# A recurrent-attention block with a mixture of experts: another order of its front, shorter routing, values projected first

## The chip, the cores and the metric

The kernel runs on one core of one Trainium2 chip. The metric is the device time of one execution in microseconds (us), given as the median of three runs; lower is better. Engine names in this text: TensorE (PE in the profile, its weight loads PEld), VectorE (DVE), ScalarE (ACT), GpSimd (POOL), SyncE (SP). "ACTq", "SPq" and "POOLq" are the sequencers of these engines, which also issue DMAs.

## The reference

The input `x` is 4 batches of 512 tokens of 256 numbers. Every row is normalised (`xn`). From `xn` two things are computed and multiplied:

```
s: RMS norm, then q, k (128 wide), v, g (256 wide), gk = log_sigmoid(xn Wkg1 Wkg2 + b)/16
   16 heads: S_t = S_(t-1) * exp(gk_t) + k_t v_t ;  o_t = q_t S_t      (a scan over 512 tokens)
   o normalised per head, times silu(g), times Wo, added to xn
   RMS norm, then x + (silu(x W1) * (x W3)) W2                        (hidden width 704)
g: 16 experts (256 -> 224 -> 256, gated by silu), the 4 with the highest router scores
   weighted by their softmax; silu of the sum
out = x + s * g
```

The 2048 tokens times 4 experts are laid out in 80 tiles of 128 slots, so that one tile belongs to one expert.

## The kernel before, in words

**Engines as programs.** Each engine has a program of its own, in a fixed order, and the programs meet at semaphores. An engine that waits holds back everything that stands behind the wait. There is no planner: the order is written out by hand.

**Preparation.** SP loads the first batch and the weights `Wv`, `Wg`, `Wq`, `Wk` (L381 to L385), ACT issues the small loads (L606 to L618), all but three of them counted on one semaphore, `small_in`. ACT waits for all of `wa_in` and `small_in` (L621, L622), rounds the scaled weights to half precision (L626, "high part"), DVE computes what was lost (L898, "low part"); each product is then three half-precision products (`triple`, L312). DVE computes the norm factors of batch 0 (`statistics`, `scales`, L851 to L874), POOL makes the normed rows (L510), PE turns them (L1215), ACT and DVE split them into high and low part (L644, L912).

**Projections.** Each batch has eight outputs, in the order Z, K, V0, V1, LG, Q, G0, G1 (L295): decay, key, two halves of value, router scores, query, two halves of gate. Z is turned by ACT and POOL into the decay (L658 to L663, L515, L648); the values are copied by DVE (L927), stored to memory by SP (L407) and read back, repeated over key dimensions (L419, `vrep`, 512 KB for a step). `STEP_ENDS` (L302) says how many of the 24 outputs of batches 1 to 3 stand before the end of each of the eight steps of batch 0.

**The recurrence.** A batch takes eight steps. In step u DVE multiplies `vrep` by the key (L951), then runs two scans (L959); POOL multiplies by the query (`product`, L529); PE sums over the key (`read_out`, L1247). The scan of step u waits for the product of step u-2 (L955), the first of a batch for the banks that ACT fills with key and decay (`next_banks`, L711).

**Iterations.** The steps of batch 0 run beside the projections. Then `turns` (L338) runs iterations 1 to 5 of eight steps: in iteration i the recurrence of batch a = i, the norm chain of batch b = i-1 and the multilayer perceptron ("MLP") of batch c = i-2. The norm chain is: turned output (step 0), squares on ACT, head factors on DVE (step 2, L1109 to L1113), normalised output (step 3, L1116), turned back and gated (step 4), `Wo` (step 5), addition, row norms and their factors (step 6, L1125 to L1132), second norm, turned and split (step 7). The MLP has six gate-and-up steps (steps 0 to 5, L1291; multiplied by DVE in `gated`, L1074) and two halves of the product with `W2` (steps 6 and 7, L1279), added by DVE in the next iteration (`add_mlp`, L1086). In iterations 4 and 5 there is no recurrence; there ACT and DVE split the 16 experts' weights (L785, L1063), one for a step, the second waiting for the first.

**Routing.** DVE does it on 16 tiles of tokens by 16 experts, between the instructions of four recurrences (L975 to L1037): best scores (L987, L989), selection, softmax, counts by two matmuls (L1266), slot of each choice. For the slot of each of the four choices there are three instructions (L1032 to L1036). `name_tiles` (L1039) finds the expert of every tile, all 80 in one partition. POOL then scatters the rows to their slots (`scatter`, L556, 64 indirect DMAs), two for a step of iterations 1 to 4.

**Filling.** The slots have first to be filled with empty rows. ACT issues 16 DMAs (L634, L700), two for a step of batch 0, each of 640 rows of 1,096 bytes; POOL waits for them in front of the first scatter (L569).

**Experts.** 80 tiles, each turned, multiplied by gate and up, gated, turned, multiplied by down (L1362 to L1382), added to memory by POOL (L586). Then the last additions and the store. The diff does not touch this part or the end.

## Time and profile before

| | us |
|---|---|
| median of 3 runs | 574.86 |
| the runs | 574.86, 577.04, 572.45 |
| the profiled execution's own time | 574.92 |
| its span, first to last instruction | 572.9 |
| PE, DVE, ACT, POOL busy | 429.3, 345.0, 230.9, 304.7 |

The profile is of one execution. Busy times are means over very different stages, so a change in one stage has to be read from the rows of that stage. In a row of the timeline the columns are the start in us from the span's start, the busy time in us, the engine, the line of the code, the operation, output and inputs, and the count where several are merged; in brackets stands the idle time of the engine in front of it and what ended it.

### The profile page before, as it was taken

The page shows a single profiled execution, that of the slowest core. Times are in us where ns is not written, and L with a number is a line of the kernel's source. Part 1 is how long each engine was busy: PE and PEld are TensorE (multiplying, and loading weights), DVE is VectorE, ACT ScalarE, POOL GpSimd, SP SyncE. Part 2 cuts the span into 40 slices and gives each one's busy share as a digit, 9 for nine tenths or more (in the row PEclk, how much of TensorE's full clock was granted, in tenths as well). Part 3 has the DMA queues.
Part 4 walks back from the last instruction along what each step waited for, and adds up shares of the span by engine and source line. Part 5 has one row for each costly group of instructions (what it writes and reads, how often), then busy time and mean ns, then how long its engine had stood idle before and what let it go on. Part 6 is the DMA issues. An engine that isn't in the chain of part 4 may idle for free.

```text
span 572.9 us, 8861 instructions
## 1 busy us (share of the span) xinstructions
PE 429.3 (75%) x2170; PEld 254.9 (44%) x2171; DVE 345.0 (60%) x613; ACT 230.9 (40%) x521; POOL 304.7 (53%) x230
## 2 busy tenths in 40 slices
PE   2479970313568798699889989999999999999400
PEld 1134320101223354255465557767767767677200
DVE  4665867999989979985755633333333333333065
ACT  0526642300133132122554525556655656566221
POOL 4052695146768468576720006656566656666535
PEclk9989996655759899899999999999999999999855
DMA  8334998745535234232988845666666666664493
GB/s 265 110 111 160 304 330 279 270 150 171 186 123 185 89 126 151 106 114 65 357 288 238 176 149 85 112 101 114 103 112 112 112 102 110 111 85 57 55 318 121
DMA packets 78616, 90.42 MB, mean 158 GB/s; under 512 B 7704, under 2 KB 66808, under 8 KB 78584
## 3 DMA queue, kind: packets, MB, share of 16 engines
q1 hardware_dynamic: 47584, 54.82, 31.6%
q0 software_dynamic: 14592, 19.47, 20.0%
q10 hardware_dynamic: 16408, 15.73, 8.5%
q8 instruction: 16, 0.26, 0.2%
q14 instruction: 16, 0.13, 0.1%
HBM read 50.66 MB, written 39.34 MB: 157 GB/s over the span
## 4 chain that ended last, share of the span: by engine, by line
PE 54%; DVE 19%; issue 9%; DMA 8%; POOL 4%; ACT 2%; ACTq 2%; SPq 0%; POOLq 0%; DVEq 0%
PE mm_ps L315 33%; PE sum_ps L315 12%; DVE st L959 4%; PE turn_ps L1276 3%; DVE kv L951 3%; PE mm_ps L1374 3%; POOL qs L529 2%; DMA rows_scratch<-zrow 2%; DMA eb<-n_L_ffn_expert_bias_dram 2%; PE sum_ps L1247 2%; DVE w_gu L1181 2%; DMA vrep<-v_scratch 1%; DMA y_scratch<-y,X 1%; ACTq L636 1%; DVE ghead L1111 1%
## 5 line engine op out<-in xcount | busy, mean ns | idle before, releaser
L586 POOL DMA_INDIRECT y_scratch<-y,X x80 | 124.3, 1554 | 126.7 <-ACT y L815 96.6
L315 PE MATMUL mm_ps<-w_gu,xT 128*128 x480 | 103.9, 352 | 1.6 <-DVEq L1159 1.5
L529 POOL TENSOR_TENSOR qs<-st,q_sb 128x1024 f32<-128x1024 f32 x32 | 75.4, 2356 | 49.0 <-DVE st L959 24.3
L1071 DVE TENSOR_TENSOR xT<-turn_ps,xT 128x256 f16<-128x256 f32 x80 | 33.9, 425 | 88.0 <-ACT xT L726 88.0
L315 PE MATMUL sum_ps<-wd,hT 112*128 x320 | 82.4, 380 | 0.0
L558 POOL DMA_INDIRECT rows_scratch<-rows,slot_u x64 | 64.0, 1001 | 27.2 <-issue 15.1
L959 DVE TENSOR_TENSOR_SCAN st<-sum_ps,kv 128x512 f32<-128x512 f32 x64 | 75.1, 1210 | 1.0
L315 PE MATMUL mm_ps<-an2T,w 128*128 128x512 f16 x264 | 65.1, 403 | 13.6 <-DVE h_mlp L1080 11.1
L1247 PE MATMUL sum_ps<-qs,sumk 128*32 128x512 f32 x128 | 38.2, 710 | 38.5 <-POOL qs L529 37.2
L315 PEld LDWEIGHTS mm_ps<-w_gu,xT 128*128 128x128 f16 x480 | 46.6, 97 | 33.0 <-issue 2.7
L1164 DVE SCALAR_TENSOR_TENSOR h<-mm_ps,X,sl 128x224 f32<-128x224 f32 x80 | 36.1, 451 | 40.9 <-ACT sl L799 40.9
L315 PEld LDWEIGHTS sum_ps<-wd,hT 112*128 112x128 f32 x320 | 54.3, 190 | 4.7 <-issue 0.2
L815 ACT ACTIVATE y<-sum_ps,X 128x256 f32<-128x256 f32 x80 | 38.0, 474 | 44.3 <-PE sum_ps L315 44.3
L799 ACT ACTIVATE sl<-mm_ps,X 128x224 f32<-128x224 f32 x80 | 35.8, 447 | 43.4 <-PE mm_ps L315 43.4
L315 PE MATMUL mm_ps<-anT,w_a 128*128 128x512 f16 x168 | 43.0, 414 | 11.2 <-DVE anT L912 9.2
L315 PEld LDWEIGHTS mm_ps<-an2T,w 128*128 128x128 f16 x264 | 26.3, 103 | 54.1 <-issue 16.6
L315 PE MATMUL mm_ps<-w,h_mlp 128*128 128x256 f32 x192 | 47.8, 394 | 1.0 <-DVE h_mlp L1080 1.0
L951 DVE TENSOR_TENSOR kv<-vrep,mm_ps 128x1024 f32<-128x1024 f32 x32 | 38.8, 1212 | 5.6 <-ACT mm_ps L677 4.1
L315 PEld LDWEIGHTS mm_ps<-w,h_mlp 128*128 128x128 f32 x192 | 33.9, 189 | 14.5 <-issue 10.0
L732 ACT ACTIVATE sg<-mm_ps 128x512 f32<-128x512 f32 (+1 forms) x24 | 14.3, 597 | 46.8 <-PE mm_ps L315 46.8
L1276 PE MATMUL turn_ps<-ident,X 128*128 128x128 f32 x160 | 30.7, 274 | 2.5 <-issue 2.5
L315 PEld LDWEIGHTS mm_ps<-anT,w_a 128*128 128x128 f16 x168 | 16.9, 105 | 34.9 <-issue 17.8
(165 smaller groups left out, 533.4 us busy)
## 6 DMA issues: line engine op xcount, KB each, us to landing
vrep<-v_scratch SPq DMA_DIRECT2D x64, 256.0 KB
rows_scratch<-zrow ACTq DMA_DIRECT2D x16, 685.0 KB, 11.7
X<-rows_scratch SPq DMA_DIRECT2D x80, 137.0 KB, 2.6
w_gu<-y_scratch SPq DMA_DIRECT2D x16, 256.0 KB, 6.1
y_scratch<-zrow ACTq DMA_DIRECT2D x6, 640.0 KB, 5.9
w_gu<-in_L_ffn_gate_proj_dram SPq DMA_DIRECT2D x16, 224.0 KB, 6.8
w_gu<-in_L_ffn_up_proj_dram SPq DMA_DIRECT2D x16, 224.0 KB, 7.1
wd<-in_L_ffn_down_proj_dram SPq DMA_DIRECT2D x1, 3136.0 KB, 17.4
```

The source lines that it names most:

```text
L315: last = nc.tensor.matmul(out_ap, lhsT, rhs, start=(n == 0), stop=(n == len(pairs) - 1))
L529: nc.gpsimd.tensor_tensor(qs[:, u % 2, :, :], st[:, u % 2, :, :], pair_bc(q_sb[:, TOK(a)]), ALU.mult).then_inc(s["qs_ready"], 1)
L558: nc.gpsimd.indirect_dma_start(rows_dram, bass.IndirectOffsetOnAxis(ap=slot_u[:, j, t:t + 1], axis=0), rows[:, t, :], None).then_inc(s["sc ...
L586: nc.gpsimd.indirect_dma_start(y_dram[u % 2], bass.IndirectOffsetOnAxis(ap=X[:, u, TOKEN_C:TOKEN_C + 1].bitcast(U32), axis=0), y[:, u, :], ...
L799: nc.scalar.activation(sl[:, u % 2, :], M[u % 2][:, 0:I], ACT.Silu, scale=X[:, u, SCALE_C:SCALE_C + 1])\
L815: nc.scalar.activation(y[:, u, :], sum_ps[:, u % 2, 0:D], ACT.Copy, scale=X[:, u, bass.ds(e + WEIGHT_C, 1)])\
L951: nc.vector.tensor_tensor(kv[:, r, :, :], vrep[:, r, :, :], pair_bc(K_BANK), ALU.mult).then_inc(s["kv_ready"], 1)
L959: nc.vector.tensor_tensor_scan(st[:, r, j, :], A_BANK, kv[:, r, j, :], 0.0, ALU.mult, ALU.add).then_inc(s["st_ready"], 1)
L1071: nc.vector.tensor_tensor(xT[:, u % 2, 1, :, :].rearrange("p c n -> p (c n)"), PS[u % 2][:, 0:KC * P], xT[:, u % 2, 0, :, :].rearrange("p ...
L1164: nc.vector.scalar_tensor_tensor(out=h[:, u % 2, :], in0=M[u % 2][:, I:2 * I], scalar=X[:, u, SCALE_C:SCALE_C + 1], in1=sl[:, u % 2, :], o ...
L1247: last = nc.tensor.matmul(O0[rows_at:rows_at + QUARTER, :], sumk[:, off:off + QUARTER], qs[:, u % 2, j, :], start=(dd % PER == 0), stop=(d ...
L1276: last = nc.tensor.transpose(PS[u % 2][:, n * P:(n + 1) * P], X[:, u, n * P:(n + 1) * P], ident[:, :])
```

## The change

1. **Preparation.** The small loads are split over several semaphores and over SP and ACT: only `ln1` and three router and decay weights stay ahead on ACT; `bkg2`, `bg`, `ln2` and the expert bias go to SP's queue, the last two behind all of `x`. Weights are prepared in the order in which they are used, and PE waits for each output's own part. The outputs come in the order V0, V1, Z, K, LG, Q, G0, G1. ACT copies the values, not DVE. The norm factors of batches 2 and 3 move behind the first recurrence.
2. **Batch 0.** `STEP_ENDS` spreads the 24 outputs evenly. All eight recurrences stand ahead of the routing.
3. **Filling.** POOL prepares, in the space of the MLP weights, ten empty rows for each partition; ACT issues 8 DMAs (one for a step) of 128 pieces of 10,960 bytes in place of 16. The preparation of the MLP weights, whose space that is, moves on POOL from batch 0 to steps 0 to 5 of iteration 1, behind a wait for all fills, which stands behind the first product.
4. **Norm chain in six steps, MLP from step 6.** Head factors and normalised output are in step 1, gating in step 2, `Wo` and addition in step 3, row factors in step 4, turning and splitting in step 5. The MLP of batch b starts in step 6 of the same iteration; iteration 5 has six steps.
5. **Routing** in three parts (steps 0, 2 and 4 of iteration 1). The slots of the four choices are the four largest of 16 slot numbers: one multiplication and 16 instructions of maxima. The expert of tile p is found in partition p; one turn by PE and one copy bring the names to one partition.
6. **Scatters** begin in step 6 of iteration 1; two and three in turn in the steps of iterations 1 to 3, three for each step of iteration 4.
7. **Experts' weights**: one expert for a step until 7 are split, then two for a step.

```diff
-        Z_OUT, K_OUT, V0_OUT, V1_OUT, LG_OUT, Q_OUT, G0_OUT, G1_OUT = range(8)
+        V0_OUT, V1_OUT, Z_OUT, K_OUT, LG_OUT, Q_OUT, G0_OUT, G1_OUT = range(8)
-        STEP_ENDS = [7, 11, 14, 17, 20, 24, 24, 24]
+        STEP_ENDS = [4, 7, 10, 13, 16, 19, 22, 24]
+        MLP_FROM = 6
             for it in range(1, B + 2):
-                for u in range(U):
-                    step_fn(batch(it), batch(it - 1), batch(it - 2), u)
+                for u in range(U if it <= B else MLP_FROM):
+                    c, m = (it - 1, u - MLP_FROM) if u >= MLP_FROM else (it - 2, u + U - MLP_FROM)
+                    step_fn(batch(it), batch(it - 1), batch(c), m, u, (it - B) * U + u)
+        def experts_at(n):
+            single = n - 2
+            if 0 <= single < 7:
+                return (single,)
+            pair = 7 + 2 * (n - 9)
+            return tuple(e for e in (pair, pair + 1) if e < E) if n >= 9 else ()
 # gpsimd
+            step(nc.gpsimd.memset(wide, 0.0))
 ...
                 product(0, u)
-                if 1 <= u <= 3 * KC:
-                    mlp_weights((u - 1) // 3, (u - 1) % 3)
-            pool.sem_inc(s["prep_done"], 1)
+                if u == 0:
+                    pool.wait_ge(s["ln_ready"], 3)
+                if u < 2:
+                    for t in range((u + 2) * TPB, (u + 3) * TPB):
+                        normed_rows(t)
 ...
                     product(a, u)
                 if b == 0 and u == 0:
+                    pool.wait_ge(s["zero_fill"], 16 * FILLS)
+                    pool.wait_ge(s["late_in"], 32)
+                if b == 0 and u < 3 * KC:
+                    mlp_weights(u // 3, u % 3)
+                if b == 0 and u == 3 * KC - 1:
+                    pool.sem_inc(s["prep_done"], 1)
+                if b == 0 and u == SCATTER_FROM:
                     pool.wait_ge(s["route_ready"], 1)
-                    pool.wait_ge(s["zero_fill"], 16 * NT)
-                if b is not None:
-                    scatter(2)
+                if b is not None and (b > 0 or u >= SCATTER_FROM):
+                    scatter(3 if b == B - 1 or u % 2 else 2)
 # scalar
-            act.wait_ge(s["wa_in"], 64)
-            act.wait_ge(s["small_in"], 16 * NSMALL)
-            act.wait_ge(s["wv_ready"], 1)
+            act.wait_ge(s["ln1_in"], 16)
+            act.wait_ge(s["wqk_in"], 32)
 ...
+                if i in (V0_OUT, V1_OUT):
+                    c = i - V0_OUT
+                    act.wait_ge(vt_out[c], 16 * (p + 1))
+                    nc.scalar.activation(vt[:, c, :], bank_of(p, i), ACT.Copy).then_inc(s["vt_ready"], 1)
 ...
-                    zero(rows_dram[t * (SLOTS // NT):(t + 1) * (SLOTS // NT)], "zero_fill")
+                fill_rows(u)
 # vector
-            for c in range(1, B):
-                statistics(c)
 ...
-            scales(TPB, NT, TPB + NT)
+            statistics(1)
+            scales(TPB, 2 * TPB, 3 * TPB)
             low_rows(1)
 ...
-            FIRST = 6
+            FIRST = U
             for u in range(FIRST):
                 for _ in recurrence(0, u):
                     pass
+                if u == 0:
+                    row_scales(TPB, 2 * TPB)
+                    statistics(2)
+                    statistics(3)
+                if u == 1:
+                    scales(2 * TPB, NT, 6 * TPB)
+                    row_scales(2 * TPB, NT)
 ...
-            for j in range(TOP):
-                step(nc.vector.scalar_tensor_tensor(out=pick[:, :, :], ...
-                step(nc.vector.tensor_tensor(prod[:, :, :], pick[:, :, :], slot[:, :, :], ALU.mult))
-                step(nc.vector.tensor_reduce(slot_f[:, j, :], prod[:, :, :], AX.X, ALU.add))
+                step(nc.vector.tensor_tensor(slot[:, :, :], slot[:, :, :], Msel[:, :, :], ALU.mult))
+                for t in range(NT):
+                    nc.vector.max(s8[:, t, :], slot[:, t, :]).then_inc(s["dve_max"], 1)
 ...
+            def step_fn(a, b, c, m, u, n):
+                split_low(experts_at(n - 1)[-1:])
+                if b == 0 and u == 5:
+                    low_of_turned(b)
+                if a is not None:
+                    for ahead in {0: (0, 1), 1: ()}.get(u, (u,)):
+                        for _ in recurrence(a, ahead):
+                            pass
+                if c and u == MLP_FROM:
+                    add_mlp(c - 1, 1)
 ...
+                if c is not None and m < NF:
+                    gated(c, m)
```

## Rows read from the trace of the kernel before

**Rows 1.** Busy time by stage: start:end, length, PE, PEld, DVE, ACT, POOL, clock, DMA
```profile
0.00:40.70 40.70, 18.16 (x90) 9.01 (x91) 23.60 (x90) 13.03 (x22) 11.89 (x34) 0.98 0.53 163
40.70:127.00 86.30, 45.79 (x262) 19.06 (x264) 68.22 (x104) 33.87 (x56) 42.51 (x26) 0.78 0.74 250
127.00:165.80 38.80, 18.29 (x56) 7.30 (x56) 35.33 (x52) 6.18 (x17) 25.75 (x18) 0.59 0.52 165
165.80:215.50 49.70, 43.70 (x178) 20.83 (x179) 45.65 (x65) 12.98 (x27) 34.59 (x25) 0.90 0.38 129
215.50:264.90 49.40, 41.82 (x183) 20.76 (x182) 46.67 (x67) 12.00 (x25) 33.34 (x25) 0.97 0.35 111
264.90:307.00 42.10, 37.62 (x172) 22.74 (x172) 23.57 (x51) 17.65 (x31) 19.97 (x19) 1.00 0.83 267
307.00:336.40 29.40, 26.88 (x119) 15.37 (x119) 16.47 (x20) 12.39 (x17) 0.00 (x0) 1.00 0.67 155
336.40:572.90 236.50, 197.01 (x1116) 139.84 (x1116) 85.48 (x174) 122.82 (x326) 136.66 (x88) 0.93 0.63 119
```

**Rows 2.** The chain that ended last, stretch 0 to 130: start, us, what
```profile
6.98 9.39 DMA eb<-n_L_ffn_expert_bias_dram
...
60.57 8.04 DMA vrep<-v_scratch
...
97.99 12.98 DMA rows_scratch<-zrow
```

**Rows 3.** Timeline of 0 to 75: first projections, factors of batches 1 to 3, first recurrence
```profile
23.25 7.92 PE L315 MATMUL mm_ps<-anT,w_a 128*128 128x512 f16 x24 [7.83 <-DVE anT L912]
...
23.31 4.01 DVE L854 BATCH_NORM_STATS2 bst<-xn 128x6 f32<-128x256 f32 x12
...
32.20 0.89 DVE L860 BATCH_NORM_AGGREGATE mv<-bst 128x2 f32<-128x6 f32 x12
...
36.33 0.42 DVE L872 SCALAR_TENSOR_TENSOR rows<-ctmp,nhalf 128x12 f32<-128x12 f32 x1
...
40.67 1.21 DVE L951 TENSOR_TENSOR kv<-vrep,mm_ps 128x1024 f32<-128x1024 f32 x1
```

**Rows 4.** Costliest groups of the page: count, busy, mean ns, idle before
```profile
L529 POOL TENSOR_TENSOR qs<-st,q_sb 128x1024 f32<-128x1024 f32 x32 | 75.4, 2356 | 49.0 <-DVE st L959 24.3
...
L558 POOL DMA_INDIRECT rows_scratch<-rows,slot_u x64 | 64.0, 1001 | 27.2 <-issue 15.1
```

**Rows 5.** Groups by line and form, whole span: DVE's expert splits and value copies
```profile
L1063 DVE TENSOR_TENSOR w_gu<-w_gu 128x896 f16<-128x896 f32 x16 | 17.4, 1086 | 3.2 <-ACT w_gu L785 3.2
...
L927 DVE COPY vt<-mm_ps 128x512 f32<-128x512 f32 x8 | 5.5, 689 | 9.5 <-PE mm_ps L315 9.5
```

**Rows 6.** Timeline of 75 to 127: routing on DVE, GpSimd's weights, a late bank
```profile
84.26 1.30 DVE L989 MAX8 m<-lg 128x8 f32<-128x16 f32 x16
...
92.19 2.85 POOL L539 TENSOR_TENSOR w<-w_raw,w 128x1408 f16<-128x1408 f32 x1
...
101.16 1.22 DVE L951 TENSOR_TENSOR kv<-vrep,mm_ps 128x1024 f32<-128x1024 f32 x1 [4.15 <-ACT mm_ps L677]
...
115.96 0.42 DVE L1033 SCALAR_TENSOR_TENSOR pick<-cnt,Msel 128x256 f32<-128x256 f32 x1
...
121.00 0.42 DVE L1036 TENSOR_REDUCE slot_f<-prod 128x16 f32<-128x256 f32 x1
```

**Rows 7.** Timeline of 120 to 300: end of routing, a stalled head factor, PE's steps
```profile
125.03 1.86 DVE L1047 TENSOR_SCALAR tile_expert<-own 1x80 uint32<-1x80 f32 x1
...
135.02 2.79 DVE L1111 TENSOR_SCALAR ghead<-ghead 128x64 f32<-128x64 f32 x1
...
182.49 0.20 DVE L1111 TENSOR_SCALAR ghead<-ghead 128x64 f32<-128x64 f32 x1
...
269.29 2.76 PE L315 MATMUL mm_ps<-an2T,w 128*128 128x512 f16 x12
...
291.98 5.93 PE L315 MATMUL mm_ps<-w,h_mlp 128*128 128x256 f32 x24
```

566 lines of the change are left out of this document (293 added, 273 removed).

## The prediction

> **What bounds the kernel now.** I read the busy times by stage first [rows 1]. The reader is to see three different kernels in them. From 336.4 on the expert tiles run (PE busy 197 of 236.5 us); the diff does not touch them, so I carry 236.5 us over. From 165.8 to 264.9 lie iterations 2 and 3: 49.7 and 49.4 us, DVE busy 45.65 and 46.67 of them, so VectorE sets their length, with PE (43.7, 41.8) just behind. From 264.9 to 336.4 PE is busy 37.62 of 42.10 and 26.88 of 29.40: there PE sets the time. What is left is the front. From 40.7 to 165.8 (125.1 us) DVE is busy 68.22 + 35.33 = 103.6 us and idle 21.5, while the clock falls to 0.59 because PE has nothing to do. Up to 40.7 nothing is full.
>
> The chain of waits shows why the start is late [rows 2]: the expert bias, issued at 6.98, lands at 16.37, and ACT and DVE wait for all small loads before they prepare any weight. PE projects from 23.25 on; the first recurrence starts at 40.67 [rows 3], after the factors of all twelve further tiles (32.20 to 36.75) and the turning of batch 1 (36.75 to 40.67). In routing, DVE once sits idle 4.15 us until ACT has filled the key bank [rows 6], since ACT is busy issuing fills.
>
> So the model is four terms: start to first recurrence; batch 0 with iteration 1; iterations 2 and 3; the tail up to the first expert tile. The sum is made against 574.92 us, the profiled execution's own time, which is the median (574.86).
>
> **Term 1, start to first recurrence.** Without the wait for the expert bias, what is still needed are the norm factors, the mean of `Wv` and the normed rows, which are there at about 12 in the timeline. Of the 6.9 us between 16.37 and 23.25 some 3.3 are left, since only the parts for V0 stand ahead: PE starts at about 15.3. Then come V0, V1, Z, K, LG. Four outputs took 7.92 us [rows 3]; five take 8.8: LG is read at 24.1. DVE adds constants and low parts (0.6), statistics of four tiles (4.01 / 3 = 1.3) and the factors (36.75 - 32.20 = 4.55, less two thirds of 0.89: 4.0), then the turning as before, 3.9. First recurrence at 33.9, against 40.67: **-6.8 us**. Bounds: at most -9.4 (the transfer that is waited for), at least -3 (SP now issues five further small DMAs ahead of the value store, and `vrep` may land late). I take -6.8, nearest to the rows. The copy of V by ACT costs nothing on the path: ACT was busy only 13.03 of 40.7.
>
> **Term 2, batch 0 and iteration 1.** What DVE loses and gains:
> - values, six copies in this stretch at 0.689 [rows 5]: -4.1;
> - slots: from 115.96 to 121.42 there are twelve instructions, 5.5 us; in their place one multiplication (0.42), 16 maxima (1.30, as for the scores) and three short ones (0.5) [rows 6]: -3.3;
> - names of tiles: 121.42 to 126.89, 5.5 us, in one partition [rows 7]; a copy of about 0.3 is left: -5.2;
> - statistics of batches 2 and 3: 4.01 x 2 / 3 = +2.7; their factors +4.6 [rows 3]; two `gated` more in iteration 1, +1.4.
>
> Busy: 103.6 - 12.6 + 8.7 = 99.7. Idle was 21.5. With 3 outputs for a step in place of 7, the idle of 4.15 for the bank gone and the routing no longer laid between recurrences, I stepped the programs: idle stays where batch 2's rows are normed, turned and split behind its late factors (about 4.5), at two score outputs (2.5) and once for PE's last outputs (3): 10. PE's work in batch 0 (38.1 busy of 42.3 before) is then as long as DVE's, so it may set some steps. Term 2 is 109.7 in place of 125.1: **-15.4 us**. Bounds: -21 (idle almost gone) and -7 (idle as before, plus one more stall).
>
> The new wait in this stretch is POOL's, for all fills, behind the first product of iteration 1 (at about 88). Queued behind it are the MLP weights (up to 2.85 each, [rows 6]) and the second product, which `read_out` and so PE's turn of the normalised output in step 2 need by about 100. The last fill is issued at about 81. One fill took 12.98 us before, behind a backlog [rows 2]; 81 + 13 = 94, so it is just hidden. From a landing at 97 on, each us costs one.
>
> Where a head factor starts beside a product it took 2.79 us, otherwise 0.20 [rows 7]; these stalls are in the busy time that I carry over. The Trainium skill says in "GPSIMD Engine Reference", Key points, that GpSimd shares its SBUF interfaces with VectorE and contends with instructions in a two-port mode or with two SBUF inputs. That agrees with those two rows, and it speaks against this change, which gives POOL more to do beside DVE (weights in iteration 1, 20 scatters for an iteration); one or two further stalls of 2.6 us would make the sum 3 to 5 us longer. That is inside my range.
>
> **Term 3, iterations 2 and 3.** DVE's work stays (46.2 on average). Three waits come in. First, in step 6 DVE adds the old MLP's second half and then wants the new MLP's first product, for which PE has waited on that very addition: 2.76 us for twelve matmuls [rows 7] plus silu, 3.1 in all with nothing between. Second, POOL: 8 products at 2.36 and 20 scatters at 1.00 + 0.25 [rows 4] are 43.9 us in place of 38.9. It is not the bound, but in steps with three scatters (6.1 us) the product comes late, `read_out` holds PE's turns behind it, and the chain loses about 3. Third, about 0.9 at the head factors, whose input now is needed one step earlier. What goes: the idle around the row factors is hidden behind a recurrence, already counted in using busy time only. An iteration is 46.2 + 3.1 + 3 + 0.9 = 53.2: for two 106.4 against 99.1, **+7.3 us**. Bounds: -2 (waits fall beside each other) and +19 (below).
>
> **Term 4, tail.** Before: 336.4 - 264.9 = 71.5. Two gate-and-up steps of the last but one MLP now lie in iteration 3, -5.5 (2 x 2.76). A half product of 5.93 [rows 7] no longer overhangs the last recurrence: -1.5. With two experts for a step, ACT and DVE in turn split for some 4.2 us (DVE's share 1.09 for each, [rows 5], ACT's about the same) in a step of 2.76: +3. The 21 scatters left at 1.27 end about 27 us in, long before the first rows are wanted. 67.5: **-4.0 us**. Bounds -7 and +3.
>
> **Sum.** -6.8 - 15.4 + 7.3 - 4.0 = -18.9: 574.92 - 18.9 = **556.0 us**. All lower bounds together give 535.5, all upper ones 587.
>
> **Rivals.**
> 1. *The waits of term 3 hide* (DVE has 3 us of idle in each iteration already, which could absorb them). Against it: the addition and the product in step 6 depend on each other directly. Iterations of 49.5: 556.0 - 7.3 = 548.7. Chance 0.2.
> 2. *GpSimd paces iterations 2 and 3.* If the four extra scatters of an iteration (5 us) lie in full on the path beside the waits, an iteration is about 59: +19 in place of +7.3, so 567.7. For it: products already wait in turn with DVE and PE (49.0 idle in all, [rows 4], half of it for DVE). Chance 0.12.
> 3. *The front gives little*: weights arrive no earlier, or the first recurrence waits for `vrep`, which once took 8.04 us beside fills [rows 2]. Term 1 is nothing: 562.8. Here the change does not do what it says. Chance 0.08.
> 4. *The fills come late* (the slower side). The eight fills have pieces ten times as long, and no row shows such pieces. If each took the 12.98 us of the last one before [rows 2], one after another from 37 on, the last would land at 141, 44 us after the point where it decides (97): about 600. It makes the kernel slower than before from a landing at 116 on. Against it: 16 fills were served in the same stretch at 250 GB/s [rows 1], overlapping. Chance 0.05. The Trainium skill ("DMA: Bandwidth & Descriptors", Queues, rings and completion order) says that each DMA engine takes turns between queues packet by packet; by that, long packets would hold back `vrep`, not themselves.
>
> **How the numbers follow.** Forecast as summed, 0.55; the rivals 0.2, 0.12, 0.08, 0.05. The likeliest case gives 556.0, its own range is 547 to 565. To leave out no more than 2 in 10, I take 543 to 569: it holds rivals 1 to 3. A measurement of this kernel tells about 1% from no change (569.1 and below is faster, 580.6 and above slower). Faster: nearly all of forecast and of rivals 1 and 3, most of rival 2: 0.87. Within 1%: 0.07. Slower: rival 4 and an unseen wait, 0.06.
>
> **What would show it.** Right: the first recurrence starts at 32 to 36; iteration 2 starts (third batch's first key product) at 138 to 148; its length is 51 to 55, with DVE idle some 3 us before `gated` of m = 0; the first expert matmul is at 311 to 323; fills land before 97 and ACT no longer waits while issuing them. Wrong: a POOL wait of over 10 us for the fills, the first recurrence after 38, iterations of 58 or more, or PE at the low clock through batch 0.

## The result, and the profile after

The changed kernel takes 594.94 us (median of 4 runs, 593.17 to 596.18) where the kernel before takes 573.65 in the same measurement: 1.036 times as long, 95% interval 1.030 to 1.042. The forecast was 556.0, range 543 to 569. The profiled execution took 596.18 us, its span is 594.0 (before 572.9).

The windows of the changed kernel, cut at the same events as [rows 1]: first recurrence, first recurrence of batch 1, of batch 2, of batch 3, end of batch 3's, last MLP, first expert product.

```profile
0.00:34.30 34.30, 18.47 (x90) 8.96 (x91) 18.19 (x71) 14.51 (x26) 12.45 (x30) 0.95 0.72 202
34.30:94.00 59.70, 45.56 (x242) 18.00 (x242) 39.10 (x67) 31.06 (x56) 24.45 (x18) 0.85 0.72 269
94.00:166.20 72.20, 32.66 (x98) 12.89 (x98) 60.51 (x122) 12.88 (x26) 32.77 (x17) 0.62 0.43 130
166.20:224.80 58.60, 46.19 (x187) 23.70 (x187) 48.59 (x67) 13.12 (x28) 38.51 (x29) 0.91 0.42 125
224.80:282.90 58.10, 46.85 (x186) 23.70 (x186) 48.61 (x66) 11.94 (x26) 38.39 (x29) 0.88 0.36 109
282.90:319.40 36.50, 30.15 (x134) 18.96 (x134) 19.20 (x43) 13.56 (x26) 23.20 (x23) 0.95 0.88 295
319.40:357.50 38.10, 31.78 (x120) 18.57 (x121) 18.20 (x22) 15.16 (x20) 0.00 (x0) 0.87 0.65 148
357.50:594.00 236.50, 196.65 (x1116) 139.51 (x1113) 86.01 (x175) 122.91 (x326) 136.67 (x88) 0.93 0.65 119
```

Read the length of each line (second number) and VectorE's busy time (the third of the busy times). In the four terms of the prediction:

| term | before | forecast | measured |
|---|---|---|---|
| 1: start to first recurrence | 40.7 | -6.8 | 34.3: -6.4 |
| 2: batch 0 and iteration 1 | 125.1 | -15.4 | 131.9: +6.8 |
| 3: iterations 2 and 3 | 99.1 | +7.3 | 116.7: +17.6 |
| 4: up to the first expert product | 71.5 | -4.0 | 74.6: +3.1 |

The expert part is 236.5, as before. Term 1 came as forecast. Term 2 is off by 22 us and term 4 by 7, both with the wrong sign; term 3 is off by 10. Of the signs that the prediction named, batch 2 starts at 166.2 (138 to 148 if right), an iteration takes 58 us or more (the sign of being wrong), and the first expert product is at 357.2 (311 to 323).

In term 2 VectorE is busy 39.10 + 60.51 = 99.6 us; 99.7 were forecast. So the sum of its instructions was right, and the whole error is idle time: 32.3 us, not 10. Its waits from 34.3 to 166.2, longest first:

```profile
DVE kv L1013 <- DMA vrep<-v_scratch: 15.4, 4, 7.2
DVE h_mlp L1141 <- issue: 7.2, 1, 7.2
DVE anT L970 <- ACT anT L686: 3.3, 2, 2.5
DVE lg L979 <- PE mm_ps L323: 3.2, 1, 3.2
```

The columns are: who, waiting for whom, total us, times, longest. The last two are the ones I had foreseen (4.5 and 2.5). The first two I had not. The first stands in the chain of what ended last, as long transfers:

```profile
61.61 15.80 DMA vrep<-v_scratch
79.30 10.74 DMA vrep<-v_scratch
91.93 8.06 DMA vrep<-v_scratch
```

A load of `vrep` that took 8.04 us once in [rows 2] now takes up to 15.80. The second is called "issue", which names nobody; the timeline around it does:

```profile
150.94 2.35 POOL L557 TENSOR_TENSOR qs<-st,q_sb 128x1024 f32<-128x1024 f32 x1 [12.98 <-DVE st L1021]
153.24 2.85 POOL L567 TENSOR_TENSOR w<-w_raw,w 128x1408 f16<-128x1408 f32 x1
156.50 4.88 PE L323 MATMUL mm_ps<-an2T,w 128*128 128x512 f16 x12 [14.30 <-POOLq L602]
161.48 0.69 DVE L1141 TENSOR_TENSOR h_mlp<-mm_ps,sg 128x512 f32<-128x512 f32 x1 [7.23 <-issue]
```

The last part of the MLP weights (L567) stands in GpSimd's program behind the product of step 5, that product behind a scan that VectorE reaches only after the slots of the routing, and PE's first MLP product behind the weights. PE has then been idle 14.30 us, and the granted clock of the next 4.9 us is 0.55, so most of them run at 1.2 GHz: twelve products take 4.88 us, not the 2.76 of [rows 7].

### The profile page after: what moved, and what is told of

It is laid out like the page before. It is cut to its first block, busy times and chain, and to the rows that moved or that the text cites. A ratio compares the mean times of both kernels' runs of the same rounds, so it can differ in the third digit from the quotient of the medians.

```text
span 594.0 us, 8877 instructions
## 1 busy us (share of the span) xinstructions
PE 448.3 (75%) x2171; PEld 264.3 (44%) x2172; DVE 338.4 (57%) x626; ACT 235.1 (40%) x531; POOL 306.4 (52%) x231
## 4 chain that ended last, share of the span: by engine, by line
PE 42%; DVE 22%; DMA 19%; issue 9%; POOL 4%; ACT 3%; SPq 1%; POOLq 0%; DVEq 0%; ACTq 0%
PE mm_ps L323 25%; DMA y_scratch<-y,X 10%; PE sum_ps L323 7%; DMA vrep<-v_scratch 7%; DVE st L1021 3%; DVE kv L1013 3%; POOL qs L557 2%; PE turn_ps L323 2%; PE turn_ps L1338 2%; PE mm_ps L1448 2%; DVE w_gu L1246 2%; PE sum_ps L1316 1%; DVE grow L263 1%; DMA w_gu<-y_scratch 1%; DVE h_mlp L1141 1%
## 5 line engine op out<-in xcount | busy, mean ns | idle before, releaser
L557 POOL TENSOR_TENSOR qs<-st,q_sb 128x1024 f32<-128x1024 f32 x32 | 75.1, 2350 | 80.9 <-DVE st L1021 80.5
L323 PE MATMUL mm_ps<-an2T,w 128*128 128x512 f16 x264 | 64.3, 398 | 16.8 <-POOLq L602 14.3
L1316 PE MATMUL sum_ps<-qs,sumk 128*32 128x512 f32 x128 | 41.6, 734 | 41.2 <-POOL qs L557 40.8
L587 POOL DMA_INDIRECT rows_scratch<-rows,slot_u x64 | 62.7, 979 | 16.9 <-issue 16.3
L323 PE MATMUL mm_ps<-w,h_mlp 128*128 128x256 f32 x192 | 55.7, 442 | 7.3 <-DVE h_mlp L1141 7.3
L323 PEld LDWEIGHTS mm_ps<-w,h_mlp 128*128 128x128 f32 x192 | 39.1, 218 | 24.0 <-DVE h_mlp L1141 9.8
L323 PE MATMUL mm_ps<-anT,w_a 128*128 128x512 f16 x168 | 45.8, 430 | 3.9 <-DVE anT L970 1.9
L1013 DVE TENSOR_TENSOR kv<-vrep,mm_ps 128x1024 f32<-128x1024 f32 x32 | 38.8, 1212 | 16.5 <-DMA vrep<-v_scratch 16.4
```

The costliest lines, as they stand in the source:

```text
L323: last = nc.tensor.matmul(out_ap, lhsT, rhs, start=(n == 0), stop=(n == len(pairs) - 1))
L557: nc.gpsimd.tensor_tensor(qs[:, u % 2, :, :], st[:, u % 2, :, :], pair_bc(q_sb[:, TOK(a)]), ALU.mult).then_inc(s["qs_ready"], 1)
L587: nc.gpsimd.indirect_dma_start(rows_dram, bass.IndirectOffsetOnAxis(ap=slot_u[:, t, j:j + 1], axis=0), rows[:, t, :], None).then_inc(s["sc ...
L1013: nc.vector.tensor_tensor(kv[:, r, :, :], vrep[:, r, :, :], pair_bc(K_BANK), ALU.mult).then_inc(s["kv_ready"], 1)
L1316: last = nc.tensor.matmul(O0[rows_at:rows_at + QUARTER, :], sumk[:, off:off + QUARTER], qs[:, u % 2, j, :], start=(dd % PER == 0), stop=(d ...
```

## The experiments

Each kernel was timed in the same set of runs as the kernel before. Unless said otherwise an edit is made to the changed kernel. In three of the five sets of runs the kernel before itself took 584 to 586 us instead of 572 to 576 (last section); there I compare by the trace up to the end of batch 3's recurrence, which that does not touch (the kernel before has 60.6, 64.6 and 49.7 in such a set). The table gives for each run the ratio and, in us, three lengths between starts of first key products (batch 0 to 1, 1 to 2, 2 to 3), and VectorE's wait for `vrep` in the first two. Each length is of one execution: e3, e5, e7 and e14, whose edits change nothing in batch 0, have 60.6 to 63.4 there where the changed kernel has 59.7, and 131.6 to 133.0 for the first two lengths together (changed 131.9). So a difference of a few us in one length is read together with the waits, not alone.

| run | ratio (95%) | 0 to 1 | 1 to 2 | 2 to 3 | vrep wait | before took |
|---|---|---|---|---|---|---|
| before | 1 | 60.5 | 64.6 | 49.7 | 0.7 | |
| changed | 1.036 (1.030-1.042) | 59.7 | 72.2 | 58.7 | 15.4 | 573.7 |
| e1 | 1.039 (1.035-1.043) | 60.3 | 71.7 | 58.9 | 4.6 | 572.5 |
| e2 | 1.030 (1.025-1.036) | 60.4 | 66.7 | 59.4 | 15.4 | 572.5 |
| e3 | 1.040 (1.036-1.043) | 60.6 | 71.2 | 58.4 | 15.5 | 572.5 |
| e4 | 1.007 (1.005-1.010) | 63.3 | 68.6 | 51.0 | 16.2 | 572.5 |
| e5 | 1.032 (1.023-1.040) | 60.7 | 70.9 | 54.0 | 15.5 | 585.8 |
| e6 | 1.017 (1.009-1.025) | 55.3 | 62.1 | 58.5 | 10.9 | 585.8 |
| e7 | 1.040 (1.032-1.049) | 63.4 | 69.6 | 58.2 | 16.2 | 585.8 |
| e8 | 1.001 (0.998-1.005) | 55.2 | 64.7 | 49.7 | 10.5 | 585.8 |
| e9 | 1.003 (1.000-1.005) | 55.2 | 60.3 | 58.3 | 1.9 | 576.0 |
| e10 | 1.033 (1.028-1.037) | 61.0 | 71.6 | 58.6 | 9.3 | 576.0 |
| e11 | 0.993 (0.991-0.996) | 54.9 | 60.6 | 53.4 | 2.2 | 576.0 |
| e12 | 0.986 (0.980-0.992) | 54.6 | 62.8 | 51.4 | 0.4 | 576.0 |
| e13 | 0.990 (0.986-0.994) | 51.3 | 63.6 | 51.0 | 2.2 | 585.8 |
| e14 | 1.057 (1.053-1.061) | 63.1 | 69.7 | 57.9 | 15.9 | 585.8 |
| e15 | 0.999 (0.996-1.002) | 49.3 | 65.1 | 49.6 | none | 585.8 |
| e16 | 1.010 (1.007-1.013) | 49.9 | 61.1 | 54.2 | none | 585.8 |
| e17 | 0.994 (0.992-0.997) | 49.1 | 65.0 | 49.5 | 0.7 | 583.5 |

### Late vrep: size of the pieces, or order of the queue

```diff
-            nc.gpsimd.iota(wide_token.bitcast(I32), pattern=[[1, WIDE], [0, 1]], base=0,
-                           channel_multiplier=WIDE).then_inc(s["wide_slot"], 1)
+            nc.gpsimd.iota(wide_token.bitcast(I32), pattern=[[0, WIDE], [0, 1]], base=0,
+                           channel_multiplier=1).then_inc(s["wide_slot"], 1)
...
-                act.dma_start(rows_dram[i * P * WIDE:(i + 1) * P * WIDE].rearrange("(p n) c -> p (n c)", p=P), wide)\
+                act.dma_start(rows_dram[i * P * WIDE:(i + 1) * P * WIDE].rearrange("(n p) c -> p n c", p=P),
+                              wide.rearrange("p (n c) -> p n c", c=ROW))\
```

> The changed kernel takes 594.9 us. Edit: the eight fills write the same 11.2 MB, but as 1,280 pieces of 1,096 bytes each in place of 128 pieces of 10,960. Theory A (long pieces on ACT's queue hold back the loads of vrep on SP's queue): DVE's wait for vrep up to the end of routing, 15.4 us in the changed kernel, falls to 5 or less, the first recurrence of batch 2 starts 9 to 12 us earlier (at 154 to 157 in place of 166.2), the time is 583 to 586. Rival B (the bytes alone count, or the loads are late because SP's queue stands behind the stores of v): the wait stays within 3 us of 15.4 and the time within 3 us of 594.9. Rival C (the pieces cost the queues more than the bytes): fills land later, POOL waits for them in iteration 1, and the time is 598 or more.

Measured: the wait for `vrep` fell from 15.4 to 4.6 us, as theory A had it, and the time did not move: 595.27. Part of that fall is hidden behind the bank below; in front of the recurrences of batch 0 alone, which stand ahead of it, the wait fell from 12.6 to 4.6, and the last of them starts at 82.4 in place of 90.1. Three rows of this run's timeline, of ACT's queue and of VectorE:

```profile
81.48 8.49 ACTq L673 DMA_DIRECT2D rows_scratch<-w  x1
90.12 4.12 ACTq L673 DMA_DIRECT2D rows_scratch<-w  x1
95.11 1.22 DVE L1014 TENSOR_TENSOR kv<-vrep,mm_ps 128x1024 f32<-128x1024 f32 x1 [9.09 <-ACT mm_ps L724]
```

One issue of 1,280 pieces held ACT's queue 8.49 us (0.34 with long pieces; the first four issues of this run, with as many pieces, took 0.4, so it is those behind a backlog that are held), and the key bank that ACT fills was 9.09 us late. The same 11.2 MB cost VectorE's loads with long pieces and the issuing engine with short ones. That is also what [rows 6] showed before: 4.15 us for the same bank, where single issues of fills held ACT's queue up to 4.90 us. A part of rival C came too: the fills landed in 14.6 us (median, 8.4 with long pieces), and GpSimd waited 8.8 us for them in iteration 1. So A's mechanism held, its time did not.

```diff
             for u in range(U):
                 load_values((u + 2) // U, (u + 2) % U)
-                for p, i in outs_at(u):
+                for p, i in outs_at(u - 1) if u else ():
                     if i in (V0_OUT, V1_OUT):
                         store_values(p, i - V0_OUT)
```

> Edit: the changed kernel, with SP storing the values of a step's outputs behind the next step's loads of vrep, not ahead of them. Theory A (the fills on ACT's queue make vrep late): the wait for vrep up to the end of routing stays at 13 to 17 us in place of 15.4, the ratio at 1.034 to 1.038. Rival B (the loads stand behind stores that wait for their projection): the longest wait, 7.2 us in front of the sixth recurrence, goes, the wait in all falls to 8 or less, the ratio to 1.020 to 1.026.

Measured: 1.033 (1.028 to 1.037). The rows of its waits look like rival B at first:

```profile
DVE kv L1013 <- DMA vrep<-v_scratch: 9.3, 3, 7.0
DVE kv L1013 <- DMA v_scratch<-vt: 6.4, 1, 6.4
```

but together they are 15.7, and the time stays: with the loads ahead, the store comes late and the load behind it. So this order does not give the wait back. As the edit itself delays the stores, it does not rule the order out as a share; what speaks against that is e9 below, where the wait goes to 1.9 us with the order as it was.

Next, the fills in a space of their own, in pieces of middle size, with the weights back in batch 0; then the same, spread.

```diff
-    FILLS = 8
-    WIDE = SLOTS // (P * FILLS)
+    FILLS = 10
+    WIDE = 2
...
-        wide = w13[:, :, :, :].rearrange("p a c n -> p (a c n)").bitcast(F32)[:, 0:WIDE * ROW]
+        wide = fill1[:, 0:WIDE * ROW]
...
-                act.dma_start(rows_dram[i * P * WIDE:(i + 1) * P * WIDE].rearrange("(p n) c -> p (n c)", p=P), wide)\
+                act.dma_start(rows_dram[i * P * 8:(i + 1) * P * 8].rearrange("(n p k) c -> p n (k c)", p=P, k=WIDE),
+                              wide.rearrange("p (a c) -> p a c", a=1).to_broadcast((P, 4, WIDE * ROW)))\
...
+                if 1 <= u <= 3 * KC:
+                    mlp_weights((u - 1) // 3, (u - 1) % 3)
```

> Edit: the empty rows come from a space of their own (two rows for a partition), in ten fills of 512 pieces of 2,192 bytes, one for each step of batch 0 and two in iteration 1; with that, GpSimd prepares the MLP weights in batch 0 again and waits for the fills only before the first scatter. Theory A (two prices, each its own: 15 us of late vrep by the long pieces, of which the smallest pieces gave back 11 but paid 9 for a key bank behind ACT's blocked issues; and 5 us by the late MLP weights, which the run with two parts for a step gave back): the pieces of middle size keep most of the first without blocking ACT, the first recurrence of batch 1 starts at 84 to 88 in place of 94, that of batch 2 at 150 to 156 in place of 166, the time is 579 to 586. Rival B (ACT's queue is blocked by 512 pieces too, or the bytes alone make vrep late): only the weights' part comes back, 588 to 591. Rival C (GpSimd's weight work beside batch 0 costs DVE stalls and late products there): 591 or more.

Measured: batch 1 starts at 88.2, batch 2 at 150.3, both where theory A put them; `vrep` still costs 10.9 us. The absolute time, 595.8, lies outside A's 579 to 586, but from the last recurrence to the experts this run takes 94.9 us where the changed kernel, in a quiet set, takes 78.4; without these 16.5 us it would be 579.3 (an estimate from these figures). The ratio is 1.017. Not all of theory A is shown by it: its edit changes size, source and place at once, and only the parts' sum is measured.

```diff
-                fill_rows(u)
+                if u in (0, 1, 3, 5, 7):
+                    fill_rows((0, 1, 3, 5, 7).index(u))
...
+                if b == 0 and u < 5:
+                    fill_rows(5 + u)
```

> Compared by the ratio to the kernel before (changed kernel 1.036, narrow version 1.017), since the runs of a job share its runs. Edit: the narrow version, with five of its ten fills in batch 0 (steps 0, 1, 3, 5, 7) and five in steps 0 to 4 of iteration 1. Theory A (what is left of late vrep, 10.9 us, is the fills' bytes beside the loads): that wait falls to 4 or less, the first recurrence of batch 1 starts at 82 to 85 in place of 88.2, that of batch 2 at 144 to 148 in place of 150.3, the ratio is 1.005 to 1.010. Rival B (vrep is late because SP issues it behind the stores of v): the wait stays at 9 to 11 and the ratio at 1.017. Rival C (the fills of iteration 1 hold the first scatter, and POOL the next products): batch 2 starts later than 150.

e9 is e6 with this edit. Measured: 1.003 (1.000 to 1.005), the wait for `vrep` 1.9 us, batch 2 at 150.0. In front of the recurrences of batch 0 the wait fell from 4.2 to 0.5: the bytes beside the loads made it. The rest of e6's wait (6.5 us at the start of batch 1) is partly hidden here by the next row in the list; e13, without that row, has 2.2 in all. But batch 1 did not start earlier (89.7), because of that row:

```profile
DVE kv L1016 <- ACT mm_ps L723: 5.4, 1, 5.4
DVE lg L982 <- PE mm_ps L323: 4.1, 2, 3.3
```

The key bank again: ACT's program has it behind the last gate outputs, for which PE is late. By the first two lengths e9 gains 0.1 + 1.8 us on e6; the ratios differ by more (0.014), but come from unlike sets.

### The weights' wait

```diff
-                if b == 0 and u < 3 * KC:
-                    mlp_weights(u // 3, u % 3)
-                if b == 0 and u == 3 * KC - 1:
+                if b == 0 and u < 3:
+                    mlp_weights(2 * u // 3, 2 * u % 3)
+                    mlp_weights((2 * u + 1) // 3, (2 * u + 1) % 3)
+                if b == 0 and u == 2:
```

> Edit: POOL prepares the MLP weights of two parts in each of the steps 0 to 2 of iteration 1, in place of one in each of steps 0 to 5. Theory A (PE's first MLP product waits 14.3 us for the last part, and DVE's first gated product 7.2 us behind it): both waits go but for the 3 us that any first product costs there, the first recurrence of batch 2 starts 4 to 6 us earlier, the time is 589 to 591. Rival B (the product of the query that now comes later in steps 0 to 2 holds back PE's turned output and the head factors, and the loss only moves): the time stays within 2 us of 594.9. Rival C: PE's first MLP product waits for something else just as long (the turned and split rows of batch 0), the start of batch 2 does not move.

Measured: 589.79, and batch 2 at 160.6 in place of 166.2. This is theory A. PE's product now waits for the rows' low part:

```profile
148.60 4.73 PE L323 MATMUL mm_ps<-an2T,w 128*128 128x512 f16 x12 [5.12 <-DVE an2T L1154]
155.44 0.66 DVE L1142 TENSOR_TENSOR h_mlp<-mm_ps,sg 128x512 f32<-128x512 f32 x1
```

### Iterations 2 and 3

In the changed kernel VectorE's waits of iteration 3 (224.8 to 282.9) and GpSimd's are:

```profile
DVE xn L1194 <- PE turn_ps L323: 3.8, 2, 2.7
DVE h_mlp L1141 <- PE mm_ps L323: 2.9, 1, 2.9
DVE xn L1148 <- PE mm_ps L323: 1.0, 1, 1.0
...
POOL qs L557 <- DVE st L1021: 18.0, 6, 4.3
```

GpSimd waits for VectorE 18.0 us, so it does not pace the iteration. The 2.9 are the wait that I forecast at 3.1. But idle time is not all. VectorE is busy 48.6 us in each of the two iterations, where I had taken 46.2, and 2.1 of these 2.4 us are one small instruction of the row factors that starts beside a GpSimd product and ends with it (without a product beside it: 0.17):

```profile
260.45 2.35 POOL L557 TENSOR_TENSOR qs<-st,q_sb 128x1024 f32<-128x1024 f32 x1 [3.46 <-DVE st L1021]
260.54 2.28 DVE L263 TENSOR_SCALAR grow<-grow 128x4 int32<-128x4 int32 x1
```

The experiments took one of the waits at a time.

```diff
-                        for _ in recurrence(a, ahead):
-                            pass
-                if c and u == MLP_FROM:
-                    add_mlp(c - 1, 1)
+                        for k, _ in enumerate(recurrence(a, ahead)):
+                            if k == 0 and c and u == MLP_FROM:
+                                add_mlp(c - 1, 1)
+                if a is None and c and u == MLP_FROM:
```

> Edit: in step 6 the addition of the old MLP's second half stands between the multiplication and the two scans of that step's recurrence, not behind them. Theory A (DVE waits 2.9 us for the first gated product because PE's first product waits for this addition): the wait in front of the first gated product falls to 1 or less, iterations 2 and 3 are 55.5 to 57 us in place of 58.4, the time is 590 to 592. Rival B (the scans then stand behind a W2 product that is not ready, or PE is the later one anyway): the wait only changes its place, the iterations keep 58 us and the time stays within 2 us of 594.9.

Measured: 595.10, iteration 2 at 58.4: rival B. The wait for the gate product went to 0.7, that for the `W2` product behind the addition rose from 1.0 to 3.4:

```profile
266.06 7.46 PE L323 MATMUL mm_ps<-w,h_mlp 128*128 128x256 f32 x24
273.56 0.69 DVE L1148 TENSOR_TENSOR xn<-mm_ps,xn 128x512 f32<-128x512 f32 x1 [3.42 <-PE mm_ps L323]
```

What I had counted as a wait for an addition is PE, busy nearly without a gap from 248 on with `Wo`, half of `W2`, the turned rows, the other half, part of it at the low clock. PE has its gaps in steps 1 and 2 (2.67 and 3.37 us) and is full in steps 3 to 6.

Ahead of `Wo` PE waits, in the changed kernel, in the sum over the key of the step before, and part of `Wo` then runs at the low clock (5.23 us at a granted 0.70; in the kernel before 3.72 at 1.00):

```profile
248.07 1.92 PE L1316 MATMUL sum_ps<-qs,sumk 128*32 128x512 f32 x4 [3.39 <-POOL qs L557]
249.92 5.23 PE L323 MATMUL turn_ps<-wo,gs 128*128 128x256 f32 x16
```

```diff
-                if a is not None and u > 0:
+                if a is not None and u > 0 and u != 3:
                     read_out(a, u - 1)
...
+                if a is not None and u == 3:
+                    read_out(a, u - 1)
```

> The changed kernel takes 594.9 us. Edit: in step 3 of each iteration PE runs the product with Wo before the sum over the key of the recurrence of step 2, not behind it. Theory A (what lengthens iterations 2 and 3 is a chain of PE and DVE: PE stands 3.4 us behind GpSimd's late product, so Wo is late and at the low clock, so DVE waits 2.7 and 1.0 us for it): PE has no wait of 3 us there, DVE's wait for Wo falls to 1.5 or less, an iteration is 55 to 56.5 us in place of 58.4, the time 588 to 591. Rival B (the later steps, the two W2 halves of 6.0 and 7.5 us between the turning and the first gate product, end last whenever Wo comes): the waits of DVE only move to the additions of steps 5 and 6, an iteration stays at 58, the time within 2 us of 594.9.

Measured by the trace: 165.2 to 219.2 to 273.4, so iterations of 54.0 and 54.2 in place of 58.6 and 58.1, one better than theory A's 55 to 56.5. VectorE's wait for `Wo` is 0.8 in place of 3.8. `Wo` itself is as slow as it was (5.41 us), so what the exchange gave is its place, not its clock; the granted clock of the two iterations is 0.97 and 0.94 in place of 0.91 and 0.88. The time, 604.15, can't be held against 588 to 591, since before took 585.8 here.

```diff
-                for u in range(U if it <= B else MLP_FROM):
-                    c, m = (it - 1, u - MLP_FROM) if u >= MLP_FROM else (it - 2, u + U - MLP_FROM)
+                for u in range(U):
+                    c, m = it - 2, u
```

and every piece of the chain goes back to the step named in the description of the kernel before. With them the experts' weights are split as before, and the names of the tiles are turned ahead of the first recurrence of batch 2, not in step 7 behind it: the edit undoes a little more than part 4.

> Edit: part 4 of the change alone is undone. The norm chain again takes eight steps, the MLP starts in the next iteration, both halves are added behind the first recurrence of the next, iteration 5 has eight steps, the experts' weights are split as before; routing, preparation, fills, scatters and weights on POOL stay as changed. Theory A (the six-step chain lengthens iterations 2 and 3 by its waits, 17.6 us, and the tail by 3): iterations 2 and 3 fall from 58.4 to 50 to 51.5 us, the tail from 74.6 to 70 to 73, the 7.2 us wait in front of the first gated product goes, and the time is 565 to 573. Rival B (GpSimd's three scatters in a step are what lengthens the iterations, by port stalls on DVE and late products): the iterations stay at 55 us or more, and the time is 583 to 592. Rival C: undoing it costs the two steps that iteration 5 saved as much as it gives, 594.9 within 3 us.

Measured: 577.28, ratio 1.007: 17.7 us less than the changed kernel's 594.94, the largest share of a single edit. The iterations are 51.0 and 51.8 us (theory A: 50 to 51.5). The time is 4 us above A's range. The wait for the weights went, but from the first recurrence to batch 2 it still takes 131.9 us, as in the changed kernel. What took its place is, for 5.0 us, the turned names of the tiles, which here stand in front of batch 2, and the row factors:

```profile
DVE tile_expert L1111 <- PE turn_ps L1370: 3.7, 1, 3.7
DVE grow L1195 <- ACT on L804: 1.3, 1, 1.3
```

The 63.3 us for batch 0 are no effect of the edit (e7 and e14 have 63.4 and 63.1). The profiled execution (583.98) was the slowest of six, so its tail is not used; its trace locates 12.2 of the 17.7 us, 13.6 less up to the end of batch 3 and 1.4 more behind it.

```diff
-                    scatter(3 if b == B - 1 or u % 2 else 2)
+                    scatter(4 if b == B - 1 else 2)
```

> Edit: the changed kernel (ratio 1.036) with two scatters for each step of iterations 1 to 3 and four for each step of iteration 4. Theory A (my term: in steps with three scatters GpSimd's product comes late, 3 us an iteration): iterations 2 and 3 fall from 58.4 to 55 to 56 us, the ratio to 1.025 to 1.030. Rival B (GpSimd has time, 38.4 busy of 58.1, and the length comes from PE's chain): the iterations stay within 1 us of 58.4 and the ratio at 1.034 to 1.038. Rival C (fewer scatters mean fewer stalls of DVE beside them): DVE busy falls from 48.6 to 47.6 or less, and the iterations by that 1 us.

Measured: iterations 57.9 and 57.7; VectorE still waits for `Wo` (4.3), the gate (2.9) and `W2` (1.1); its busy time is 47.7 in place of 48.6. So rival B with C's small part: the third scatter of a step, 3 us in my term, costs at most 1. PE's wait for GpSimd's product ahead of `Wo` stays too (4.26 us): that product is not held by scatters, it starts when VectorE's scan ends. In eight steps iteration 2 takes 51.0 us in e13 and 49.6 in e15, which differ in the scatters alone; but e8, with the scatters of e13, has 49.7, so this difference shows nothing. The ratio, 1.057, lies outside all theories; the loss is in iteration 4, in the stall told below, which is longest in this run (29.5 us), with four scatters in a step; e15 and e16 with as many have 17.4 and 25.3.

### The tail

```diff
-            if 0 <= single < 7:
+            if 0 <= single < 10:
                 return (single,)
-            pair = 7 + 2 * (n - 9)
-            return tuple(e for e in (pair, pair + 1) if e < E) if n >= 9 else ()
+            return {12: (10, 11, 12), 13: (13, 14, 15)}.get(n, ())
```

In the changed kernel the pairs of experts made PE wait, and a good part of its `W2` products then ran at the low clock (granted 0.71; 1.00 in the run below). The first product of the last MLP, then the `W2` products, in the kernel before and in the changed one:

```profile
307.01 14.40 PE L315 MATMUL mm_ps<-an2T,w 128*128 128x512 f16 x66 [0.83 <-issue]
322.83 12.00 PE L315 MATMUL mm_ps<-w,h_mlp 128*128 128x256 f32 x48 [0.97 <-DVE h_mlp L1080]
...
319.44 14.40 PE L323 MATMUL mm_ps<-an2T,w 128*128 128x512 f16 x66 [0.83 <-issue]
339.03 16.61 PE L323 MATMUL mm_ps<-w,h_mlp 128*128 128x256 f32 x48 [4.75 <-DVE h_mlp L1141]
```

> Edit: the experts' weights are split one for a step up to the tenth, and the last six in the two steps of the W2 products, none in pairs beside the last gate steps. Theory A (the pairs of ACT and DVE, 2.17 us for an expert in turn, delay the last two gated products by about 4 us, so PE waits 4.75 us and its W2 products run at the low clock, 16.6 us in place of 12): both go, the first expert product comes 6 to 9 us earlier, the time is 586 to 589. Rival B (the splits at the end then hold back the first expert tile as much): within 2 us of 594.9. Rival C (the wait goes but the clock stays low): 590 to 592.

Measured, with the experts moved:

```profile
355.24 12.00 PE L323 MATMUL mm_ps<-w,h_mlp 128*128 128x256 f32 x48 [0.97 <-DVE h_mlp L1140]
373.15 2.42 PE L323 MATMUL mm_ps<-w_gu,xT 128*128 x6 [5.91 <-DVEq L1223]
```

Both costs went, 3.8 and 4.6 us, and a wait of 5.9 (before: 1.5) came in front of the first expert product: the splits at 2.17 us each were not done. From the first product of the last MLP to the first expert product it takes 33.7 us in place of 37.7, a gain of 4.0, between A's 6 to 9 and B's 2 at most. The ratio, 1.040 (1.032 to 1.049), comes from a set with the stall and can't settle it.

### Versions put together

Their edits are those above, but for three. The experts of e11 (`experts_at`), the banks of e13, e15, e16 and e17 (`next_banks` moved up, its old call gone), and the scatters of e17 (e15 and e16 have e14's):

```diff
+            return {2: (0,), 3: (1, 2), 4: (3, 4), 5: (5, 6), 13: (14, 15)}.get(n, (n + 1,) if 6 <= n <= 12 else ())
...
             for u in range(U):
+                if u == U - 1:
+                    next_banks(0)
                 for p, i in outs_at(u):
...
-                    scatter(3 if b == B - 1 or u % 2 else 2)
+                    scatter(3 if b in (0, B - 1) or b == 1 and u >= SCATTER_FROM else 2)
```

e8 (the edits of e4 and e6):

> Edit: the undone part 4 (norm chain in eight steps again, 577.3 us alone) together with the fills and the weights of the narrow version. Theory A (the front's losses are independent of the order of the norm chain; the weights' wait was not there in eight steps): 10 us of late vrep come back on top of the 17.6, and the time is 564 to 569, under both kernels. Rival B (only part of it is on the path, as the next engine in the front is PE at 45 busy of 60 us): 569 to 573. Rival C (ACT is blocked in its issues): 575 to 578.

Measured: 1.001 (0.998 to 1.005), 587.1 beside 585.8. By the trace batch 2 starts at 152.9 and its iteration takes 49.7: the two gains add up, which is A's mechanism (the first two lengths are 12 us shorter than e4's). Its time is not shown: without the stall (95.3 us from the last recurrence to the experts, 78.5 in e12) it would be 570.3, an estimate, and that is in rival B's range.

e11 (six steps with the edits of e5, e6, e9 and the experts' new places):

> Edit: the norm chain in six steps as changed, with narrow and spread fills, weights in batch 0, Wo ahead of the sum over the key in step 3, and the experts' weights split in pairs in iteration 4 (steps 3 to 5) and singly beside the gate steps. Theory A (the prices found are each other's neighbours, not the same one): front 22 us and two iterations 9 us less than the changed kernel, PE does not wait 4.75 us ahead of the last W2 products and they take 12 us: the tail 8 us less. In all 36 to 40 us less, a ratio of 0.966 to 0.974. Rival B (in the tail the splits of iteration 4 only move the wait into the norm chain of the last batch): 0.975 to 0.985. Rival C (a new bound in the front, PE at 44 busy of 55 us): 0.985 to 1.0.

Measured: 0.993 (0.991 to 0.996), 571.94 us, a ratio in rival C's range. The front is e9's (the key bank, 5.3 us), iteration 2 is 53.4; the way from the last recurrence to the experts is 80.5 us, not shorter than the changed kernel's 78.4. The new places of the experts did at the end what A says (`W2` 12.00 us behind a wait of 0.97; 33.1 us from the last MLP's first product to the experts in place of 37.7), but the way from the last recurrence to that product became 47.4 us in place of 40.7: that is where rival B puts the loss, and in sum nothing is gained.

e12 (the edits of e4, e6 and e9):

> Edit: the norm chain in eight steps, with narrow and spread fills and weights in batch 0. Theory A (eight steps keep iterations of 50 us, six steps save two steps at the end): the front 5 us less than in the narrow version of eight steps (1.001), a ratio of 0.990 to 0.994, behind the six-step version with its own waits gone. Rival B (six steps cost the iterations more than they save whatever is mended): this version is the faster of the two.

Measured: 0.986 (0.980 to 0.992), 567.65 against 575.95 us. It is under A's 0.990, and A's order of the two versions was wrong, rival B's right. It is faster than both kernels, by 1.4% (0.8 to 2.0) than the kernel before.

e13 (e12 with early banks):

> Edit: the eight-step version with spread fills (ratio 0.986), with ACT filling the banks of key and decay for batch 1 ahead of the last two gate outputs of batch 3, not behind them. Theory A (the 5.3 us in front of the first recurrence of batch 1 are the key bank alone): the wait goes, batch 1 starts at 82.5 to 84 in place of 87.9, batch 2 at 145 to 147 in place of 150.7, the ratio is 0.977 to 0.980. Rival B (vrep for that recurrence, or PE's sums over the key that stand behind the late gate outputs, then end last): batch 1 starts earlier, but batch 2 does not, the ratio stays at 0.984 or more.

Measured: 0.990 (0.986 to 0.994), with before at 585.8. By the trace the 5.3 us in front of batch 1 went, 1.4 for `vrep` came; batches 0 to 1 take 51.3 us in place of 54.6, 1 to 2 take 63.6 in place of 62.8: 2.5 us in single executions, about half of A.

e15 (e13 with e14's scatters):

> Edit: eight steps, spread fills, early banks and two scatters for a step. Theory A (both prices are real in eight steps too): 5 us from the banks and 2 to 4 from iterations 1 to 3, a ratio of 0.970 to 0.975. Rival B (the scatters cost nothing): 0.977 to 0.980. Rival C (four scatters for a step make iteration 4 GpSimd's and the scatters end later than the experts can wait): above 0.980.

Measured: 0.999 (0.996 to 1.002). The last recurrence starts at 242.1 us (before: 260.2), but from there to the experts it takes 105.5 us in place of e13's 95.6: rival C's place, by the stall.

e16 (six steps with the edits of e5, e6, e9, early banks and e14's scatters):

> Edit: six steps, spread fills, early banks, Wo ahead of the sum over the key, two scatters for a step, the experts' pairs as in the changed kernel. Theory A (six steps keep iterations 3 us longer than eight have them, the tail gives back 4 at most): a ratio of 0.978 to 0.988, above the eight-step version by 0.005 or more. Rival B (with the scatters gone the six-step iterations are as short): the two are within 0.003.

Measured: 1.010 (1.007 to 1.013), 0.011 above e15, which is A's order and distance. It missed A's range; from the last recurrence to the experts it takes 105.9 us, with the stall in it. What this run does show is the front: with `vrep`, the weights and the bank mended, batch 0 and iteration 1 take 49.9 + 61.1 = 111.0 us, where I had forecast 109.7 for term 2.

e17 (e13 with nearly even scatters):

> Edit: eight steps, spread fills, early banks; two scatters for a step, three in iteration 4, in the last two steps of iteration 1 and in the last two of iteration 2. Theory A (the gains of the spread version, 0.986, of the early banks, 2.5 us, and of the even scatters, 1.4 us for each of iterations 2 and 3 and 2.7 for the last, add up, and three scatters for a step in iteration 4 do not lengthen the tail): a ratio of 0.974 to 0.980. Rival B (what the front and the iterations give goes to the tail, where the experts' weights and the scatters wait for each other): 0.984 to 0.990.

Measured: 0.994 (0.992 to 0.997), 580.8 against 583.5 us. Its last recurrence starts at 241.1 us, 8 before e12's and 19 before that of the kernel before, and its tail has the stall. That it would be some 8 us under e12 in a set without the stall is worked out from these rows, not measured.

## Why the prediction was wrong

- **Term 1** was right: -6.4 for -6.8.
- **Term 2, busy time** was right to 0.1 us: the values' copies, the maxima (1.32 for 1.30) and the named tiles gave what the rows said. That the sum fits this well is partly luck: small instructions slowed beside GpSimd (2.79 at a head factor before) are others now (2.24 at a row factor, 2.96 at L1063), and they happen to add up to as much.
- **Term 2, idle time**, is the step that failed ("idle stays where batch 2's rows are normed ... 10"). It was 32.3. My upper bound of -7 was added up wrongly too: with the busy time at 99.7, "idle as before" (21.5) alone gives 121.2, or -3.9. I stepped the engines and left the queues out. 15.4 us of it is late `vrep`. I had even named its mechanism, but as a remark on rival 4: that long packets "would hold back `vrep`, not themselves". The Trainium skill ("DMA: Bandwidth & Descriptors", Queues, rings and completion order) says that each DMA engine takes turns by packets; e1 fits that, with 12.6 us of waits in batch 0 for long pieces and 4.6 for short; e9 shows that the amount of bytes beside the loads counts as well. The fills themselves landed in 8.4 us (median; 9.0 at most) and GpSimd never waited for them, so rival 4's wait did not come: its victim was another.
- The other part, 7.2 us, is a program order on GpSimd. I listed the MLP weights as queued behind the wait for fills, but did not ask who waits for the last of them: PE's first MLP product, which the change moves from iteration 2 to step 6 of iteration 1. e2 took back 4.8 us (127.1 for the first two lengths in place of 131.9). With both causes and the late bank mended, the stretch takes 111.0 us (e16), near the forecast's 109.7.
- **Term 3** was 10.3 us short. Of that, 4.8 are busy time: the stall at the row factors, 2.1 us an iteration, which I had named ("one or two further stalls") and left out of the sum. The other 5.5 are idle time, 10.0 and 9.5 us an iteration for my 7. The wait at the first gate product came (2.9 for 3.1), but it was not a price of its own (e3). The second wait had its second half right and its cause wrong: the sum over the key does hold PE's next work behind GpSimd's product (3.39 us ahead of `Wo`), but not because of three scatters (e14). What I had not added up is PE: six steps put `Wo`, both halves of `W2` and the turned rows behind one another in steps 3 to 6. e5 took back 4 us an iteration by one exchange, e4 6 to 8. Rival 2 named the right length (59 us) with the wrong engine.
- **Term 4**: the saved steps came nearly as forecast, 36.5 us for iteration 4 after 42.1: -5.6, where I had -5.5 and -1.5. The mis-sized part is the pairs of experts, taken at +3. From the first product of the last MLP to the first expert product it takes 37.7 us, before 29.4: +8.4, and that is the wait (4.75 for 0.97) and the slower `W2` products (16.61 for 12.00).
- **The chances**: slower than before by over 1% had 0.06, and came; 0.05 of that stood for rival 4, whose wait did not.

## What to carry to other kernels

When a transfer is made of larger pieces, ask which other queue's loads wait beside it; when it is made of smaller ones, ask what stands behind the issue on the engine that issues it. The best answer here was pieces of middle size and half of the bytes at another time. When a chain is folded into fewer steps, add up the work of every engine step by step in the new order: a mean of 46 busy of 58 us hid four full steps behind two with gaps. And when one wait is removed, read which row stands next in the list of waits before adding the gain to a sum.
